# The last router of a four-layer kernel: its second half cut into two quarters, one routed beside the attention

## What is computed

```python
x = x + _L3_xattn_ref(_layernorm(x), ctx, ...)          # 16 heads over 77 context rows, then Wo
xf = _layernorm(x).reshape(N, D)                        # N = 2048 tokens
eid = argmax(softmax(xf @ router_w + router_b))         # one of 8 experts a token
rank = cumsum(onehot(eid), axis=0)[token, eid] - 1      # place among the tokens of that expert
valid = rank < 320
buf = zeros((8, 320, D)).at[eid, where(valid, rank, 0)].add(xf * valid)
y = relu(buf @ w1 + b1) @ w2 + b2                       # per expert, 256 -> 1024 -> 256
out = y[eid, pos] * valid + (relu(xf @ ow1 + ob1) @ ow2 + ob2) * (1 - valid)
x = x + out
```

## Time and profile before

| | |
|---|---|
| median of 3 runs | 1045.55 us (1042.49 to 1046.89) |
| the profiled execution: own time | 1039.85 us |
| its span | 1038.1 us |
| PE busy | 88% of the span |
| DVE busy | 69% |
| ACT, POOL busy | 36%, 37% |
| last stage `moe3` | 827.14 to the end |
| PE clock over the span | 0.956 of full |

### The profile page before, as it was taken

The page is one execution under the profiler, slowest core; times in us unless marked ns, Lnnn a source line. Parts: engine busy times, 40 slices in busy tenths (PEclk is TensorE's granted clock), DMA queues, the critical chain, the costliest instruction groups (busy, mean ns, idle before and its releaser), DMA issues. The chain is left out here.

```text
span 1038.1 us, 17090 instructions
## 1 busy us (share of the span) xinstructions
PE 912.5 (88%) x5815; PEld 648.8 (63%) x5821; DVE 713.1 (69%) x1580; ACT 377.0 (36%) x851; POOL 382.1 (37%) x281
## 2 busy tenths in 40 slices
PE   3899979999889995876899989999998829999997
PEld 2677744444467773753478557777766617777787
DVE  5688858878778886878377799999988532221212
ACT  2466641000145554861555233333332212212122
POOL 1466512433456651607455313333333320110111
PEclk9899989999989997987999999999999969999999
DMA  5000059999600005402366371111111176525200
GB/s 176 2 1 0 1 179 294 333 310 314 217 1 1 0 1 148 119 1 94 113 189 204 127 240 50 49 49 50 50 49 36 51 257 238 181 83 182 93 13 19
DMA packets 87256, 117.14 MB, mean 113 GB/s; under 512 B 12464, under 2 KB 75949, under 8 KB 86781
## 3 DMA queue, kind: packets, MB, share of 16 engines
q1 hardware_dynamic: 77455, 88.15, 27.6%
q10 hardware_dynamic: 4408, 15.46, 4.4%
q0 software_dynamic: 5328, 12.70, 3.4%
HBM read 68.08 MB, written 50.16 MB: 114 GB/s over the span
## 5 line engine op out<-in xcount | busy, mean ns | idle before, releaser
L925 PE MATMUL psum<-m_W,lnT 128*128 128x512 f32 x256 | 114.3, 599 | 0.0
L405 POOL TENSOR_TENSOR prob<-prob,a_rden 128x1232 f32<-128x1232 f32 x32 | 71.9, 2248 | 80.7 <-DVE a_rden L477 80.7
L925 PEld LDWEIGHTS psum<-m_W,lnT 128*128 128x128 f32 x256 | 47.2, 190 | 58.3 <-issue 57.3
L2730 ACT ACTIVATE prob<-psum,x_b 128x320 f32<-128x320 f32 x64 | 33.8, 527 | 124.8 <-PE psum L2784 124.8
L2412 PE MATMUL psum<-g_VW,pT 128*128 128x256 f32 (+1 forms) x320 | 73.4, 384 | 1.6 <-ACT pT L2317 1.6
L910 POOL TENSOR_TENSOR m_masked<-m_rel,m_mrow 128x1232 f32<-128x1232 f32 x16 | 43.2, 2706 | 78.5 <-DMA masked_bias<-m_masked 59.7
L2784 PE MATMUL psum<-x_xT,x_w 128*128 128x320 f32 x256 | 70.6, 434 | 1.3 <-DVE x_xT L2657 1.3
L2588 POOL DMA_INDIRECT out_x<-x_yt,x_X x20 | 19.8, 991 | 135.5 <-DVE x_yt L2671 135.5
L2412 PEld LDWEIGHTS psum<-g_VW,pT 128*128 128x128 f32 (+1 forms) x320 | 59.5, 190 | 12.6 <-ACT pT L2317 5.1
L2105 POOL TENSOR_TENSOR g_qr<-g_t 128x1024 f32<-128x1024 f32 x15 | 35.4, 2360 | 75.4 <-DVE g_t L2182 75.4
L2784 PEld LDWEIGHTS psum<-x_xT,x_w 128*128 128x128 f32 x256 | 48.3, 190 | 21.9 <-issue 2.7
(11 more groups left out here) (442 smaller groups left out, 2063.0 us busy)
## 6 DMA issues: line engine op xcount, KB each, us to landing
routed_rows<-hole SPq DMA_DIRECT2D x8, 2210.0 KB, 34.4
masked_bias<-m_masked ACTq DMA_DIRECT2D x16, 616.0 KB, 8.1
g_bias<-masked_bias SPq DMA_DIRECT2D x16, 616.0 KB, 3.8
x_w<-in_L_ffn_w SPq DMA_DIRECT2D x16, 512.0 KB, 4.5
x_w<-in_L_ffn_w SPq DMA_DIRECT2D x8, 1024.0 KB, 7.9
m_xb<-routed_rows SPq DMA_DIRECT2D x39, 130.0 KB, 2.2
m_rel<-in_rel_bias ACTq DMA_DIRECT2D x8, 616.0 KB, 10.4
expert_rows<-hole SPq DMA_DIRECT2D x1, 4680.0 KB, 33.6
```

What stands on the lines that cost most here:

```text
L405: nc.gpsimd.tensor_tensor(heads(c.prob[b]), heads(c.prob[b]), rden[b][:, :].unsqueeze(2).to_broadcast([P, H, SK]), ALU.mult).then_inc(norm ...
L925: last = nt.matmul(c.ps[p][:, :], c.lnT[b][:, k * P:(k + 1) * P], W[:, k, p * 512:(p + 1) * 512], start=(k == 0), stop=(k == KC - 1))
```

## The change

`ROUTED` names three groups of tiles in place of two halves: tiles 0 to 7, 8 to 11, 12 to 15. The functions of the router take their widths from `group_of`. The group 8 to 11 is routed in `attn_gqa`: its variances and standard deviations in step 12, its layer norms in step 13, transposes and copies in steps 13 and 14, its logits in step 15, its ranks and slots in steps 15 and 16. POOL issues the scatters of tiles 8 and 9 at the end of that stage, and those of tiles 10 and 11 at the start of `moe3`. The group 12 to 15 is routed in `moe3`, as the whole second half was. ACT evaluates one `Exp` of a spare column behind each `Sqrt` at steps 8 and 12. The unread matmuls behind the wait for all scatters are 9, not 12. The table of all statistics is still computed over 16 tiles at the start of `moe3`.

```diff
+ROUTED = [(0, HALF), (HALF, NT // 4), (HALF + NT // 4, NT // 4)]
+def group_of(u):
+    lo, n = ROUTED[u]
+    return n, slice(lo, lo + n), slice(lo * 8, (lo + n) * 8)
...
+def logits_copy(c, r, u, bank):
+    rows = ROUTED[u][1] // 2 * RW
+    return c.nc.scalar.activation(r.lgT[u % 2][0:rows, :], bank[0:rows, 0:2 * P], ACT.Copy)
...
-ROUTED_AT = {HALF + 1: (0, 1, 2), HALF + 2: (3, 4, 5), HALF + 3: (6, 7)}
+ROUTED_AT = {HALF + 1: ((0, 0), (1, 1), (2, 2)), HALF + 2: ((3, 0), (4, 1), (5, 2)), HALF + 3: ((6, 0), (7, 1)),
+             HALF + 5: ((8, 1), (9, 2)), HALF + 6: ((10, 0), (11, 1))}
```

POOL, in the attention:

```diff
+            if t == NT - 1:
+                pool.wait_ge(s["r_slot_ok"], 2)
+                for k in range(HALF, HALF + 2):
+                    scatter_tile(c, r, k)
```

DVE, in the attention:

```diff
-            if t == HALF + 1:
-                dve.wait_ge(s["r_std_ok"], 1)
-                chain(nv.reciprocal(c.rstd[:, batch0], c.std[:, batch0]))
-                for k in range(HALF):
+            if t in (HALF + 1, HALF + 5):
+                u = (t - HALF) // 4
+                _, ones8, _ = group_of(u)
+                dve.wait_ge(s["r_std_ok"], u + 1)
+                chain(nv.reciprocal(c.rstd[:, ones8], c.std[:, ones8]))
+                for k in range(ones8.start, ones8.stop):
...
+            if t == HALF + 6:
+                row_statistics(c, 1)
+            if t == HALF + 7:
+                dve.wait_ge(s["r_back_ps"], 2)
+                first_expert(c, dve, r, 1, c.ps[4][:, 0:2 * P], chain, s["r_lg_read"], 2).then_inc(s["r_oh_ok"], 1)
...
+            if t == HALF + 7:
+                first_slot(c, r, 1, chain)
+                dve.wait_ge(s["r_pre_ps"], 2)
+                slots(c, dve, r, 1, c.ps[0], chain, s["r_pre_read"], 2).then_inc(s["r_slot_ok"], 1)
```

ACT, in the attention:

```diff
+            if t == HALF + 7:
+                act.wait_ge(s["r_lg_ps"], 2)
+                logits_copy(c, r, 1, c.ps[3]).then_inc(s["r_lgT_ok"], 1)
...
+            if t in (HALF, HALF + 4):
+                u = (t - HALF) // 4
+                _, ones8, _ = group_of(u)
+                act.wait_ge(s["r_ve_ok"], u + 1)
+                na.activation(c.std[:, ones8], c.ve[:, ones8], ACT.Sqrt).then_inc(s["r_std_ok"], 1)
+                na.activation(spare[:, :], c.ones[:, 0:1], ACT.Exp)
```

PE, in the attention:

```diff
+            if t == HALF + 7:
+                pe_logits(c, r, 1, c.ps[3]).then_inc(s["r_lg_ps"], 1)
+            if t == NT:
+                pe.wait_ge(s["r_oh_ok"], 2)
+                pe.wait_ge(s["s_used"], NT)
+                pe_ranks(c, r, 1, c.ps[0]).then_inc(s["r_pre_ps"], 1)
...
+            if t == HALF + 7:
+                pe.wait_ge(s["r_lgT_ok"], 2)
+                pe_logits_back(c, r, 1, c.ps[4]).then_inc(s["r_back_ps"], 1)
```

POOL and PE in `moe3`; all else there is the same code with `range(LAST, NT)`, group 2 and `LAST` = 12:

```diff
+            for k in range(HALF + 2, LAST):
+                scatter_tile(c, rt, k)
             pool.wait_ge(s["slot_ok"], 1)
-            for k in range(HALF, NT):
+            for k in range(LAST, NT):
                 scatter_tile(c, rt, k)
...
-            keep_warm(c, c.ps[3], 12)
+            keep_warm(c, c.ps[3], 9)
```

More of the change, by code:

```diff
@@ L1051, in first_slot, with slots @@
     nv = c.nc.vector
-    pre, first = r.pre, c.first[:, u * HALF:(u + 1) * HALF]
-    if u == 1:
-        last_tile = slice((PAD + HALF - 1) * 8, (PAD + HALF) * 8)
+    n, ones8, _ = group_of(u)
+    pre, first = r.pre, c.first[:, ones8]
+    if u > 0:
+        last_tile = slice((PAD + ROUTED[u - 1][1] - 1) * 8, (PAD + ROUTED[u - 1][1]) * 8)
         for v in range(2):
             chain(nv.tensor_copy(pre[v][:, (PAD - 1) * 8:PAD * 8], pre[1][:, last_tile]))
-    chain(nv.tensor_scalar(r.slotf, first, -float(CAP), float(E3 * CAP), ALU.mult, ALU.add))
-def slots(c, dve, r, u, ranks, chain, read):
+    chain(nv.tensor_scalar(r.slotf[:, 0:n], first, -float(CAP), float(E3 * CAP), ALU.mult, ALU.add))
+def slots(c, dve, r, u, ranks, chain, read, nth=1):
     nv = c.nc.vector
     tiles = lambda t: t.rearrange("p (i g) -> p i g", g=8)
[L1064 to L1069, removed]
+    n, ones8, eights = group_of(u)
+    pre, hot = r.pre, c.gates[:, eights]
+    data = slice(PAD * 8, (PAD + n) * 8)
+    back = lambda m: slice((PAD - m) * 8, (PAD + n - m) * 8)
+    before, rank8, over8 = (t[:, 0:n * 8] for t in (r.before, r.rank8, r.over8))
+    rank, valid, orank, slotf = (t[:, 0:n] for t in (r.rank, r.valid, r.orank, r.slotf))
+    nv.tensor_copy(before, ranks[:, 0:n * 8])
+    nv.tensor_copy(pre[0][:, data], ranks[:, n * 8:2 * n * 8]).then_inc(read, 1)
+    dve.wait_ge(read, nth)
     chain(nv.tensor_tensor(pre[1][:, data], pre[0][:, data], pre[0][:, back(1)], ALU.add))
@@ L1072, in slots @@
     chain(nv.tensor_tensor(pre[1][:, data], pre[0][:, data], pre[0][:, back(4)], ALU.add))
[L1073 to L1083, removed]
+    chain(nv.tensor_tensor(rank8, before, pre[1][:, back(1)], ALU.add))
+    chain(nv.tensor_scalar(over8, rank8, -float(CAP), 0.0, ALU.add, ALU.max))
+    chain(nv.tensor_tensor(rank8, rank8, hot, ALU.mult))
+    chain(nv.reduce_sum(orank, tiles(over8), AX))
+    chain(nv.reduce_sum(rank, tiles(rank8), AX))
+    chain(nv.tensor_scalar(orank, orank, float(E3 * CAP), None, ALU.add))
+    chain(nv.tensor_scalar(valid, rank, float(CAP), None, ALU.is_lt))
+    chain(nv.tensor_tensor(slotf, slotf, rank, ALU.add))
+    chain(nv.tensor_tensor(slotf, slotf, orank, ALU.subtract))
+    chain(nv.tensor_tensor(slotf, slotf, valid, ALU.mult))
+    return nv.tensor_tensor(r.slot[:, ones8], slotf, orank, ALU.add)
 def pe_logits(c, r, u, bank):
     nt = c.nc.tensor
+    lo, n = ROUTED[u]
     for k in range(KC):
-        for g in range(GROUPS):
-            t0 = (u * HALF + 2 * g) * P
+        for g in range(n // 2):
+            t0 = (lo + 2 * g) * P
             last = nt.matmul(bank[g * RW:(g + 1) * RW, 0:2 * P], r.rw[:, k, :],
@@ L2717, in _ @@
             act_std(c, act, s["ve_ok"], s["std_ok"])
-            for n, k in enumerate(range(HALF, NT)):
+            for n, k in enumerate(range(LAST, NT)):
                 act.wait_ge(s["lnT_ps"], n + 1)
@@ L2722, in _ @@
             act.wait_ge(s["lg_ps"], 1)
-            na.activation(rt.lgT[1][:, :], bank_lg[:, 0:2 * P], ACT.Copy).then_inc(s["lgT_ok"], 1)
+            logits_copy(c, rt, 2, bank_lg).then_inc(s["lgT_ok"], 1)
             act.wait_ge(s["w_in"], 16 * 5)
```

77 lines of the change are left out of this document (38 added, 39 removed).

## The result

The changed kernel takes 1115.42 us (median of 4 runs, 1114.87 to 1118.07) where the kernel before takes 1046.22 (4 runs, 1042.49 to 1046.94): a ratio of 1.067, 95% interval 1.064 to 1.071. The forecast of 1041.4 was wrong by 74 us. The profiled execution took 1115.18, its span is 1113.4, 75.3 us above the span of before.

A forecast was written before the change was run, and what follows sets the result against it. The prediction took the router chain up to 859.58, then PE matmuls, as the bound. It summed -5.9 - 0.3 + 0.9 + 1.2 = -4.1 us, from 1045.55 to 1041.4, range 1037.3 to 1045.8.

The forecast's parts named there:

- The step that failed: From 859.58 to the end: PE matmuls, fed in time, so whatever moves 859.58 moves the end one for one.
- The second step: Attention's end, step 16: scatters of tiles 8 and 9 (2.5 us) end at about 825.8, beside DVE's last residual, free.
- Last stage: From the router to the first rows: last scatter lands 5.9 us sooner, fewer unread matmuls win 0.3 us.
- The landing: Sign in the last stage: last scatter lands 19.2 us behind the stage's start, where it was 25.1.
- The last scatter: Sign in the last stage: its issue comes about 15.2 us behind the stage's start.
- Rival 1: Last stage: weights don't hold back scatters; landing 2.44 us behind issue, -7.5 us, total 1039.8; chance 0.17.
- The rows came last: Behind the landing: rows ready after 5.0 us, nine unread matmuls after 4.0, so the rows are last; 0.3 us won.
- The clock at `hidden`: First `hidden` in the last stage: PE may start at 1.2 GHz after idle gaps; +0.9 us, bounds 0 and 2.5.
- The attention's end: Attention steps 12 to 16: added routing work costs +1.2 us in sum, bounds 0.5 and 2.5.
- Step 12's variances: Attention step 12: seven small DVE instructions, 1.0 us, inside 1.89 us of idle, cost nothing.
- Rival 2: Attention: PE's clock falls later, both `output`s of tiles 14 and 15 run cold; +9.2 us, total 1050.7; chance 0.06.
- rival 3: Attention queueing costs 2.5 us without the clock, `hidden` starts cold at 2.5; total 1044.4; chance 0.17.

The follow-up runs named there:

- e2_scatters_late: `e1_count` with the scatters of tiles 8 and 9 issued at the start of the last stage, not the attention's end: 1044.51 us, ratio 0.999.
- e8_one_scatter: `e1_count` with only tile 8 scattered in the attention, tile 9 at the last stage's start: one execution, drain ends at 839.6.
- e4_late_weights: `e2_scatters_late` with the second expert's weights queued behind the wait for all scatters and the first expert's rows: 1041.20 us, ratio 0.9965.
- e1_count: The changed kernel with the overflow count adding a column of zeros instead of the carried count: 1048.48 us, ratio 1.0047.
- e6_warm_gap: `e4_late_weights` with 12 unread matmuls, not 9, and four more between the transposes and the first `hidden`: 1038.80 us, ratio 0.995.
- e10_again: `e6_warm_gap` measured a second time, unchanged, on the same chip: 1035.36 us, ratio 0.9953.
- e11_nine_gap: `e4_late_weights` with its 9 unread matmuls kept and four more between the transposes and the first `hidden`: 1036.05 us, ratio 0.9955.
- e5_warm12: `e4_late_weights` with 12 unread matmuls behind the wait for all scatters, not 9: 1042.68 us, ratio 0.9983.
- e3_before_13_blocks: The kernel before with the floor of the number of overflow blocks at 13, not 2: 1110.14 us, ratio 1.063.
- e7_ranks: `e6_warm_gap` with three unread matmuls, not eight, between ranks and transposes of tile 15 in step 16: 1039.15 us, ratio 0.9961.
- e9_before_late_gap: The kernel before, without the split, with late second-expert weights and four unread matmuls ahead of the first `hidden`: 1042.05 us, ratio 0.9997.

## Why the prediction was wrong

**The step that failed, worth 65 of the 75 us.** The forecast says that "from 859.58 to the end of its work the chain is PE matmuls, fed in time. So whatever moves 859.58 moves the end, one for one", and prices only what is moved. It took the work behind as given. But its last part is a loop whose number of rounds is a value from the router, and the changed group width altered that value. Reading the order could not show it (the loop stands there once, with the same instructions), nor could any row of before. Reading the arithmetic would have: for each function that took a new width, ask what the columns hold that are read behind it. The diff between the two kernels has the line, and the forecast did not price it. Among the rivals there was none that the change computes something else.

**The second step, worth 4 to 5 us, hidden under the first.** "The scatters of tiles 8 and 9 behind them (2.5 us) end at about 825.8, when DVE is at the last residual (now 825.5). Free too." The issues do end then (831.35, DVE's last residual at 832.43). What counts for the next stage is POOL's drain, which ended 6.7 us behind them. The row that says so, the drain at the barrier, was in the trace of before, but hidden behind DVE; I had not looked at the barrier's own instructions. `e2_scatters_late` and `e8_one_scatter` show it.

**A late start has a cost of its own.** PE stood still for the longer wait. Its first unread matmuls of the stage ran at 1.2 GHz (9 in 4.4 us against 10 in 2.3 in `e4_late_weights`), and the first copy on ACT came 4.8 us behind the stage's start, where it was 2.9.

**Last stage: right, with two small errors that cancel.** The landing was to be 19.2 us behind the start and is 20.9, of which 1.9 is the cold start: without it -6.1, forecast -5.9. The last scatter was to be issued 15.2 us behind the start; it is 15.8 in every trace from `e4_late_weights` on that has the split and no late start (17.5 less 1.9 here). And it took 3.37 us to land, not the 4.0 of the scatter it was likened to. Rival 1 (scatters not held back) is refuted, and the trace says why. The queues of after in 856 to 857 and 857 to 858, with scatters issued at 853.30, 854.57 and 855.83:

```profile
q1 hardware_dynamic: 381, 0.39, 109.5%
```

```profile
q1 hardware_dynamic: 295, 0.30, 84.6%
q0 software_dynamic: 26, 0.11, 26.2%
```

In the first of them, with the weights queued, not one packet of q0 moves. The Trainium skill, DMA: Bandwidth & Descriptors, section Queues, rings and completion order, has the engines take turns between queues; in this trace they don't, or the scatters' packets weren't yet there to be taken. Other windows point both ways. With the queue free a scatter moved 42 packets within 0.7 us of its issue (before, issue at 849.78, window 850.0 to 850.5). In `e4_late_weights` the two queues did share, with 95 packets of q0 and 101 of q1 in 841.5 to 843, as the Trainium skill has it; but in 838 to 840 of that trace q0 moved none, with four scatters issued by 837.8 and q1 at 46% of the engines. So the weights may not be all that holds a scatter back, and which of the two it is stays open. `e4_late_weights` has what rival 1 named as its condition: with the weights away the last scatter lands 0.9 to 1.3 us sooner behind its issue. The rows came last, as said: `x_XL` ends at 865.20, the unread matmuls at 864.54.

**The clock at `hidden`: mis-sized and with the wrong mechanism.** +0.9 was forecast, +1.7 measured in the changed kernel and +3.0 in `e1_count` and `e4_late_weights`, beyond the bound of 2.5. I had asked whether it would have risen by then. It had, at 864 (0.69 in 864 to 865, 1.00 in the next three windows). It fell again behind the transposes: in `e4_late_weights` in the gap, in the changed kernel just behind the first matmuls of `hidden` (0.51 in 868 to 869). I had no row for that.

**The attention's end: mis-sized, and its own trace hid it.** +1.2 was forecast, within 0.5 to 2.5, and the trace of the changed kernel has +1.76 (the last `bn_stats` at 832.96, less 6.34, against 824.86). But seven other traces with the split and the eight unread matmuls (`e1_count`, `e4_late_weights` to `e6_warm_gap`, `e8_one_scatter`, `e10_again`, `e11_nine_gap`) have 45.99 to 46.01 us from the logits of step 12 to the last `bn_stats`, against 45.88 in the trace of before: +0.1, outside the bounds. (The other two traces without the split have 45.83 and 46.64.) The 1.76 looked like a hit and was luck. What differs is the clock at the scores of tile 15 and the logits behind them, here of the changed kernel and of `e10_again`:

```profile
812.01 3.17 PE L2433 MATMUL psum<-g_KB,g_qT 128*128 128x154 f32 x16 [2.29 <-ACT lnT_all L2362]
815.11 1.88 PE L1106 MATMUL psum<-lnT_all,qT 128*32 128x256 f32 x8
```

```profile
805.35 2.36 PE L2429 MATMUL psum<-g_KB,g_qT 128*128 128x154 f32 x16 [2.29 <-ACT lnT_all L2358]
807.65 1.06 PE L1106 MATMUL psum<-lnT_all,qT 128*32 128x256 f32 x8
```

In the changed kernel's trace the granted clock was 0.50 in 814 to 816, which costs 0.8 us in each of the two. In the trace of before it had fallen there too, and the scores took 3.29 us. The scores do start later with the copies ahead of them, by 0.6 to 0.7 us against step 12's logits, as forecast; in the seven traces they run 0.9 us shorter than before and give that back. The forecast took the clock of that stretch as given.

Step 12's variances are hidden: of the 1.89 us of idle time 0.87 are left. At tile 15 PE is last, by 0.46 to 0.47 us in the seven traces; in the changed kernel's it is 1.3 (transposes at 825.50, end of DVE's division 824.21), where the forecast said up to 0.9. Rival 2 (both `output`s cold) did not happen: both take 4.59 us. Of rival 3 the cold `hidden` came and the attention's queueing did not.

**The range.** Its upper end doesn't follow from its own terms: rival 3 at 1044.4 and one microsecond are 1045.4, not 1045.8. It makes no difference here.

## What to carry to other kernels

When a change alters the size of a group, price the moved instructions, but read first what every value computed from that group is used for. A loop bound that is data is a term of the sum, and the quickest look at a large difference is the count of instructions (POOL's `ln` x13 against x4), from the end backwards. Work moved to the end of an engine's program is free only if the engine's drain at the barrier is hidden too: look for the barrier's rows, even where they cost nothing yet. And a change can be right and measure wrong: here the split gives some 0.5%, once the count, the two scatters, the weights' place in the queue and one gap of 1.3 us are put right. And a term that one trace confirms can still be that execution's clock: the attention's +1.76 against +0.1 in seven others.

## What the runs showed of the hardware that I had not expected

- POOL's drain at the barrier ended 6.5 to 6.7 us behind the end of its last indirect DMA's issue, in the twelve traces read here; how many scatters stood in the last row (one, two or five) made no difference.
- A gap of 1.33 us on PE, just behind another of 0.7 to 1.6, was followed by a fall of the clock from 2.4 GHz to 1.2 GHz in four traces with 9 unread matmuls ahead (`e1_count`, `e4_late_weights` and `e8_one_scatter` in the gap, the changed kernel about half a microsecond behind its end). It didn't in the trace of before (12 ahead, and no other gap) and in `e5_warm12` (12 ahead, the other gap 1.04), nor in `e11_nine_gap`, with 9 ahead and 0.47 us in place of the 1.33.
- The last of a row of scatters landed 2.44 us behind its issue with the queue free (2.44 to 2.67 in the traces of before, `e3_before_13_blocks`, `e4_late_weights` to `e7_ranks` and `e9_before_late_gap` to `e11_nine_gap`), 3.4 to 3.7 when the weights ended some one and a half to two and a half microseconds behind that issue, and the scatter of 842.20 in the kernel before, with the weights on the queues until about 845, 4.0.
- In the attention the granted clock fell at the scores of tile 15 in some executions and not in others of the same code there: the scores took 3.17 us in the changed kernel's trace and 2.36 in `e10_again`. The kernel before shows the same kind of spread (3.29 in its own trace, 4.03 in `e9_before_late_gap`).
